# Layer 1 of a four-layer graph kernel: attending over the activations before the projection, logits from VectorE

## The reference, cut to what matters

```
h = relu(layernorm(x));  x = x + L0(h)    # deg*(h Wi + b) + A (h Wj)
h = relu(layernorm(x));  x = x + L1(h)
h = relu(layernorm(x));  x = x + L2(h)    # as L1, with W of 256x128; output and h W side by side
h = relu(layernorm(x));  x = x + L3(h)    # 8 heads: q, k, v, softmax, output projection

L1:  Wh = h W;  e_src = Wh a_src;  e_dst = Wh a_dst
     logits[n, m] = leaky_relu(e_src[n] + e_dst[m], 0.2), -inf where A[n, m] = 0
     out = softmax(logits) Wh
```

## Time and profile before

| | |
|---|---|
| median of 3 runs | 1220.35 us |
| the profiled execution | 1220.8 us |
| its span, first to last instruction | 1218.8 us |
| TensorE (PE) busy | 1200.7 us, 99% |
| ScalarE (ACT) busy | 1082.4 us, 89% |
| GpSimd (POOL) busy | 1068.4 us, 88% |
| VectorE (DVE) busy | 1053.9 us, 86% |
| granted TensorE clock, mean | 0.999 of full speed |
| DMA | 78.57 MB, 64 GB/s on average |

### The profile page before, as it was taken

The page is one execution under the profiler, slowest core; times in us unless marked ns, Lnnn a source line. Parts: engine busy times, 40 slices in busy tenths (PEclk is TensorE's granted clock), DMA queues, the critical chain, the costliest instruction groups (busy, mean ns, idle before and its releaser), DMA issues.

```text
span 1218.8 us, 43750 instructions
## 1 busy us (share of the span) xinstructions
PE 1200.7 (99%) x12017; PEld 1108.6 (91%) x12017; DVE 1053.9 (86%) x5142; ACT 1082.4 (89%) x3976; POOL 1068.4 (88%) x1848
## 2 busy tenths in 40 slices
PE   8999999999999999999999999999999999999997
PEld 7789999999999999999999999999999999999986
DVE  6898898898898898888988988988988888988874
ACT  3679898898898898898998998998998998998997
POOL 5998899899899898999899899899899899898774
PEclk9999999999999999999999999999999999999999
DMA  7333333343442433534333332432433343330001
GB/s 187 63 46 51 77 68 55 79 67 57 77 67 57 77 67 55 79 64 60 77 63 60 77 65 58 75 68 59 71 69 60 69 67 66 67 51 26 20 20 36
DMA packets 97678, 78.57 MB, mean 64 GB/s; under 512 B 31648, under 2 KB 89248, under 8 KB 97440
## 3 DMA queue, kind: packets, MB, share of 16 engines
q1 hardware_dynamic: 94960, 74.07, 32.9%
q10 hardware_dynamic: 2480, 1.71, 0.5%
HBM read 58.79 MB, written 16.95 MB: 62 GB/s over the span
## 4 chain that ended last, share of the span: by engine, by line
PE 90%; issue 1%; DVE 1%; POOL 0%; ACT 0%; POOLq 0%; DVEq 0%; ACTq 0%
PE bank L1565 16%; PE bank L1567 16%; PE bank L1566 16%; PE bank L1715 9%; PE bank L1670 6%; PE bank L1575 6%; PE bank L1707 6%; PE bank L1727 5%; PE bank L1646 4%; PE bank L1662 3%; PE bank L1626 2%; POOL probs L469 0%; ACT exps L1315 0%; DVE masked L874 0%; PE bank L1654 0%
## 5 line engine op out<-in xcount | busy, mean ns | idle before, releaser
L1315 ACT ACTIVATE exps<-masked,nmax 128x128 f32<-128x128 f32 x1024 | 396.8, 393 | 0.9 <-DVE nmax L874 0.4
L469 POOL TENSOR_TENSOR probs<-exps,rsum 128x512 f32<-128x512 f32 x256 | 266.3, 1042 | 16.2 <-DVE rsum L882 15.7
L440 POOL TENSOR_SCALAR y<-x,nm,rstd 128x256 f32<-128x256 f32 x384 | 212.0, 560 | 31.5 <-issue 31.0
L874 DVE CUSTOM_DVE_ANT_0 masked<-bank,mask 128x128 f32<-128x128 f32 x1024 | 227.4, 284 | 0.8 <-PE bank L1707 0.5
L1315 ACT ACTIVATION_READ_ACCUMULATOR exps<-masked,nmax 128x1 f32 x1024 | 197.3, 193 | 0.0
L760 DVE BATCH_NORM_STATS2 stats<-x 128x6 f32<-128x256 f32 x512 | 190.4, 414 | 4.6 <-DMA x<-in_x 4.4
L1565 PE MATMUL bank<-w_hi,ht_hi 128*128 128x512 f32 (+1 forms) x508 | 189.4, 373 | 0.4 <-DVE ht_lo L821 0.3
L417 POOL TENSOR_TENSOR rstd<-veps,power 128x2 f32<-128x2 f32 x256 | 182.7, 714 | 5.3
L1567 PE MATMUL bank<-w_hi,ht_lo 128*128 128x512 f32 (+1 forms) x508 | 172.6, 340 | 0.0
L1566 PE MATMUL bank<-w_lo,ht_hi 128*128 128x512 f32 (+1 forms) x508 | 172.5, 340 | 0.0
L1323 ACT ACTIVATE probs3t<-bank 128x512 f32<-128x512 f32 x256 | 145.0, 595 | 0.7 <-PE bank L1715 0.7
(11 more groups left out here) (136 smaller groups left out, 3970.4 us busy)
## 6 DMA issues: line engine op xcount, KB each, us to landing
x<-in_x SPq DMA_DIRECT2D x64, 256.0 KB, 5.9
xt_sb<-in_xt SPq DMA_DIRECT2D x64, 256.0 KB, 5.7
out<-x SPq DMA_DIRECT2D x64, 256.0 KB, 5.7
db<-rows SPq DMA_DIRECT2D x110, 128.0 KB, 4.1
mean_b<-rows SPq DMA_DIRECT2D x62, 128.0 KB, 3.4
rows<-dst SPq DMA_DIRECT2D x110, 1.0 KB, 3.6
rows<-mv SPq DMA_DIRECT2D x62, 1.0 KB, 5.8
probs<-in_w0t ACTq DMA_DIRECT2D x1, 256.0 KB, 3.5
```

The lines of the kernel that those rows point to most:

```text
L440: last = pool.tensor_scalar(y[i][:, b, g], src[:, bx, g], nm[i][:, s, g:g + 1], rstd[i][:, s, g:g + 1], ALU.add, ALU.mult)
L469: pool.tensor_tensor(probs3[:, p % BUFFERS["probs3"], j], exps3[:, p % BUFFERS["exps3"], j], rsum3[:, s, j].unsqueeze(2).to_broadcast([P, ...
L874: last = dve.tensor_tensor_reduce(masked3[:, b, j, i], bank_of(f"sc{j}")[:, i * P:(i + 1) * P], mask[:], scale=-1.0, scalar=-MASKED, op0=A ...
L1315: last = act.activation(exps3[:, b, j, i], masked3[:, p % BUFFERS["masked3"], j, i], ACT.Exp, bias=nmax3[:, s, j, i:i + 1], scale=-1.0, ac ...
```

## The change

Layer 1 is computed the other way round. GpSimd makes y1 = max(x1 - mean, 0), not yet divided by the deviation (`centre1`, which does not wait for `rstd1`). W a_src and W a_dst are made once, as rows spread over all partitions, in PSUM bank 6, which nothing else uses from then on. VectorE takes each node's two logits as dot products of y1 with these rows (`logit_products1`, 4 instructions of 256 columns, each with a running sum), GpSimd multiplies the 4 columns by the inverse deviation (`scale_logits1`), and SyncE sends the a_dst part from there. The exps are scaled by the inverse deviation of the neighbour as ScalarE copies their transposed form (`copy_exp_transposed1`, now two instructions of 128 columns). TensorE multiplies y1 by them, 4 products of 128 columns whose result is already transposed (`aggregate1`, g1), ScalarE and VectorE split it, and TensorE multiplies by w1, 12 products of 256 columns (`project1`). The transposition of y1, the copies to `wh` and the gather of `dst` for layer 1 are gone. The key bias moves from VectorE to ScalarE (`add_key_bias`, 2 instructions). x1 and y1 get a third buffer. The orders of all engines, the LAG table and the banks are new; the rotating banks are 0 to 5.

```diff
-    "h1t": (6, "h1t", ('h1t_lo',)),
-    "x3b": (4, "x3_mm", ('x3',)),
-    "sc3": (4, "scores", ('nmax3_3',)),
+    "g1": (3, "g1_mm", ('g1_lo',)),
+    "x3b": (1, "x3_mm", ('x3',)),
+    "sc3": (1, "scores", ('nmax3_3',)),
+        a1_rows = bank[6]
...
+            def centre1(p):
+                b, s, bx = p % BUFFERS["y1"], p % SMALL, p % BUFFERS["x1"]
+                passed(pool, "nm1", p)
+                read_before(pool, "y1", p, "dots1", "g1_mm")
+                for g in range(G):
+                    last = pool.tensor_scalar(y[1][:, b, g], x1[:, bx, g], nm[1][:, s, g:g + 1], 0.0, ALU.add, ALU.max)
+            def scale_logits1(p):
+                passed(pool, "dots1", p)
+                passed(pool, "rstd1", p)
+                passed(pool, "z1", p, SMALL)
+                pool.tensor_tensor(logits1[:, s], dots1[:, s], rstd[1][:, s].unsqueeze(1).to_broadcast([P, 2, G]), ALU.mult).then_inc(S["sd1"], 1)
...
+            def logit_products1(p):
+                passed(dve, "y1", p)
+                dve.wait_ge(S["products"], 1)
+                for g in range(G):
+                    for k in range(2):
+                        last = dve.tensor_tensor_reduce(products1[:, k, g], a1_rows[:, k * D:(k + 1) * D], y[1][:, b, g], scale=1.0, scalar=0.0,
+                                                        op0=ALU.mult, op1=ALU.add, accum_out=dots1[:, s, k, g:g + 1])
...
-            def copy_projection1(g, p):
-                act.activation(wh[:, b, g], bank_of(f"wh{g}")[:, 0:D + 2], ACT.Copy).then_inc(S[f"wh{g}"], 1)
+            def high_g1(p):
+                act.activation(ht1_r[0][:, b].rearrange("p c g n -> p (c g n)"), bank_of("g1")[:], ACT.Copy).then_inc(S["g1_hi"], 1)
+            def copy_exp_transposed1(p):
+                for g in range(G):
+                    last = act.activation(at[1][:, b, g], bank_of("at1")[:, g * P:(g + 1) * P], ACT.Copy, scale=rstd[1][:, s, g:g + 1])
+            def add_key_bias(p):
+                for c in range(DC):
+                    last = act.activation(kt[:, b, c], bank_of("kt")[:, c * G * P:(c + 1) * G * P], ACT.Identity, bias=bk_sb[:, c:c + 1])
...
+            def aggregate1(p):
+                passed(pe, "at1", p)
+                bank_free(pe, "g1", p)
+                for c in range(DC):
+                    for g in range(G):
+                        last = pe.matmul(bank_of("g1")[:, (c * G + g) * P:(c * G + g + 1) * P], y[1][:, b, g, c * P:(c + 1) * P], at[1][:, bt, g],
+                                         start=True, stop=True)
...
-                for c in range(DC):
-                    last = split_matmul(bank_of(f"wh{g}")[:, 0:D + 2], [h_[:, b, c, g] for h_ in ht1_r], [w_[:, c, :] for w_ in w1_r],
-                                        c == 0, c == DC - 1)
+                for g in range(G):
+                    for c in range(DC):
+                        last = split_matmul(bank_of("x2b")[:, g * D:(g + 1) * D], [h_[:, b, c, g] for h_ in ht1_r], [w_[:, c, :] for w_ in w1_r],
+                                            c == 0, c == DC - 1)
```

More of the change, by code:

```diff
@@ L287, in fill @@
                 load(3)
+                load(4)
                 write_means(2)
@@ L290, in fill @@
                 spread_means(2)
-                load(4)
                 write_means(3)
@@ L368, in _ @@
             fill()
-            for t in range(17, NP + 12):
+            for t in range(15, NP + 10):
                 step(t)
@@ L701, in _ @@
             fill()
-            for t in range(9, NP + 4):
+            for t in range(6, NP + 2):
                 step(t)
@@ L1194, in _ @@
             fill()
-            for t in range(11, NP + 6):
+            for t in range(11, NP + 7):
                 step(t)
@@ L1283, in sum_logits @@
                         logits = db[i][:, p % 2].rearrange("p (n g) -> p g n", g=G)[:, g]
-                    last = act.activation(bank_of(f"zz{i}")[:, (G + g) * P:(G + g + 1) * P], logits, ACT.Prelu, bias=src[:, bs, g, col:col + 1], alpha=SLOPE)
+                    last = act.activation(bank_of(f"zz{i}")[:, (G + g) * P:(G + g + 1) * P], logits, ACT.Prelu, bias=own[:, g:g + 1], alpha=SLOPE)
                 last.then_inc(S[f"z{i}"], 1)
@@ new lines, in fill @@
+                copy_projection2(1)
+                sum_logits(2, hh[:, (1) % BUFFERS["hh"], :, F1], 1)
+                copy_exp_transposed1(3)
+                high_mj(1, 6)
+                relu_transposed_high(3, ht3_r, last_of("kt_mm", "qt_mm", "v_mm"), 0)
+                exps(2, "rsum2", 1)
+                high_mj(0, 6)
+                high_g1(3)
+                add_key_bias(0)
+                copy_exp_transposed(2, 1)
+                relu_transposed2(2)
+                sum_logits(1, logits1[:, (4) % SMALL, 0], 4)
@@ new lines, in step @@
+                if due(t, "exp3_2"):
+                    exps3_of(2, t - LAG["exp3_2"])
+                if due(t, "exp2"):
+                    exps(2, "rsum2", t - LAG["exp2"])
+                if due(t, "z1"):
+                    sum_logits(1, logits1[:, (t - LAG["z1"]) % SMALL, 0], t - LAG["z1"])
+                if due(t, "kt"):
+                    add_key_bias(t - LAG["kt"])
+                if due(t, "at2"):
+                    copy_exp_transposed(2, t - LAG["at2"])
+                if due(t, "ht2"):
+                    relu_transposed2(t - LAG["ht2"])
@@ L1647, in project2, with spread_dst @@
                 last.then_inc(S["hh_mm"], 1)
-            def spread_dst(i, src, buffer, ready, col, p):
-                b = p % BUFFERS[buffer]
+            def spread_dst(i, own, ready, p):
                 passed(pe, ready, p)
@@ new lines, in fill @@
+                project0(0, 8)
+                project_transposed("qt", wq_r, 2)
+                project_transposed("kt", wk_r, 2)
+            def drain():
+                transpose_p3(0, NP - 4)
+                transpose_p3(3, NP - 4)
+                transpose_exp(2, NP - 1)
+                transpose_p3(1, NP - 3)
+                attend(2, hh, "hh", F1, NP - 1)
+                scores(NP - 2)
+                attend3(NP - 4)
+                project_v(NP - 2)
+                transpose_y(3, NP - 1)
+                transpose_p3(2, NP - 3)
@@ L1878, in step @@
             def step(t):
+                if due(t, "d1") and at_an_end(t - LAG["d1"]):
+                    spread_dst(1, logits1[:, (t - LAG["d1"]) % SMALL, 1], "sd1", t - LAG["d1"])
+                if due(t, "g1_mm"):
+                    aggregate1(t - LAG["g1_mm"])
+                if due(t, "h2t"):
+                    transpose_y(2, t - LAG["h2t"])
+                if due(t, "e2t"):
+                    transpose_exp(2, t - LAG["e2t"])
+                if due(t, "pt3"):
+                    transpose_p3(3, t - LAG["pt3"])
+                if due(t, "pt0"):
+                    transpose_p3(0, t - LAG["pt0"])
+                if due(t, "x3_mm"):
+                    attend(2, hh, "hh", F1, t - LAG["x3_mm"])
+                if due(t, "hh_mm"):
+                    project2(t - LAG["hh_mm"])
+                if due(t, "scores"):
+                    scores(t - LAG["scores"])
+                if due(t, "ot_mm"):
+                    attend3(t - LAG["ot_mm"])
+                if due(t, "x2_mm"):
+                    project1(t - LAG["x2_mm"])
+                if due(t, "v_mm"):
+                    project_v(t - LAG["v_mm"])
+                if due(t, "pt2"):
+                    transpose_p3(2, t - LAG["pt2"])
+                if due(t, "s0"):
+                    aggregate(t - LAG["s0"])
+                if due(t, "h3t"):
+                    transpose_y(3, t - LAG["h3t"])
+                if due(t, "pt1"):
+                    transpose_p3(1, t - LAG["pt1"])
+                if due(t, "e1t"):
+                    transpose_exp(1, t - LAG["e1t"])
                 if due(t, "m1"):
```

1277 lines of the change are left out of this document (587 added, 690 removed), and 26 rows, old and new, of the table LAG.

## The result

The changed kernel takes 1240.44 us (median of 4 runs, 1239.01 to 1244.67) against 1220.68 us for the kernel before in the same session: a ratio of 1.0167 with the 95% interval [1.0141, 1.0194]. It is 1.7% slower. The forecast was 1199 us with a range of 1190 to 1213. The profiled execution took 1239.31 us, its span 1237.2.

What follows compares the result with a forecast made beforehand. TensorE was taken to set the pace, at 18.36 us a step. Span 1218.8 - 26.2 (steps) + 1.0 (prologue) + 4 (fill and drain) = 1197.6 us, which gave a time of 1199 us, range 1190 to 1213.

Steps and rivals of the forecast that it cites:

- GpSimd, per pair: GpSimd's list per pair: gather gone, four-column product added, y1 unchanged in size; loop 17.7 us, between 17.5 and 18.0.
- VectorE's dot product: VectorE, layer 1's logits: 0.34 us each, between 0.21 and 0.42; four make 1.36 us per pair.
- (b): Rival: the time stays, needing a step of 18.3 us or fill and drain longer by 20 us; chance 0.06.
- Hand-offs: Waits between engines: all fit, the a_dst row included, so nothing was charged in steady steps.
- the margin that the prediction named: At the scores after layer 2's attention, whose bank VectorE must first empty: 0.2 to 0.3 us, taken as existing already.
- The term that I had at +4: Fill and drain: 3 us for dot products in the fill, 1 for ScalarE in the drain; +4 us (0 to 10).
- What TensorE saves in all: TensorE, per pair: -0.41 us, making the step 17.95 us; 64 pairs give -26.2 us.
- (a): Rival: the other engines set the pace, by GpSimd's loop or late ScalarE; step 18.1 us, time 1208 us; chance 0.21.
- (c): Rival: with bank 6 given away, TensorE waits for six rotating banks; decides from 0.41 us per step, 1249 us; chance 0.09.
- (d): Rival: VectorE's dot products slow it, from 0.73 us each on; at 0.8 us the time is 1242 us; chance 0.04.

Runs made afterwards that it cites:

- e1: The changed kernel with layer 1's y1 in the old `add, mult` form on GpSimd, layer 1's ReLU left out: 1223.03 us.
- e11: The changed kernel, slow `max` form kept, with SyncE issuing the load of x ahead of the writing of layer 2's row: 1232.01 us.
- e8: e1 with SyncE issuing the load of x ahead of the writing of layer 2's row: 1214.75 us.
- e10: e8 with the key bias moved back from ScalarE to VectorE, right behind the query bias: 1240.41 us.
- e6: The changed kernel with layer 1's y1 on ScalarE, two `Relu` activations a pair with the negative mean as bias: 1250.37 us.
- e9: The changed kernel with y1 split, GpSimd centring graph 0 and ScalarE graph 1, and x loaded ahead of layer 2's row: 1225.61 us.
- e3: The changed kernel with layer 1's y1 made on VectorE, in front of its dot products: 1272.69 us.
- e5: The changed kernel with extra instruction forms on GpSimd and VectorE behind its last pair, timed singly and together; no kernel time given.

## Why the prediction was wrong

The step that failed is in "GpSimd, per pair": "The y1 line has the same size." The size is the same, and the form is not. I had the duration of `add, mult` and gave it to `add, max`, without bounds of its own, on the engine that I had just found to have the least slack. The rows gave no upper end for it. I looked for the nearest row and two ends where VectorE's dot product was concerned, and not here. The form adds 2 x (1154 - 557) = 1.19 us per pair to my 17.7. The run shows a loop of 18.28, so the rest of the list was shorter than I had it, about 17.1. That was luck: idle time of GpSimd's own ahead of its y instructions fell from 31.0 us in all to 10.8, and ahead of x3_tail from 10.2 to 0.7, where I had counted on little more than the second. With the 17.7 the step would be 18.9. A step of 18.3 is that of rival (b), to which I gave 0.06; with the stalls and the deeper pipeline on top the time went past it.

The distance from the forecast, 1240.4 - 1199.2 = 41.2 us, by the runs:

- The `max` form: 17.4 us (after to e1). By the cut spans about half of it is in the loop (1013.2 to 1004.9) and half in the start (120.4 to 112.7); e11 to e8 shows the same, 121.0 to 113.1. In the second 60 us GpSimd is at 54.70 with the slow form and at 55.60 without, so it has little room in either; the chain through the start was not followed.
- The late rows: 8.3 us (e1 to e8). In "Hand-offs" the a_dst row "takes 3.6 us out and 4.1 us back and has some 12 us". For layer 1's row the 12 us hold (11.8), and though it takes 5.1 out it was never late. The late one is layer 2's, which has 9.0 us and stands nowhere in the prediction. Its medians are 3.8 and 3.8, and they say nothing of the ten spreads over 6 us. Nor had I asked what shares the queue with it. The reordering of SyncE's list was in the change, and I charged it nothing.
- The step: 18.13 on average in e8 against 17.99, and with the 55 steps of the cut 7.8 us. About 0.07 of the 0.15 in an unstalled step is at the scores. From layer 2's projection to the next transposition it was 0.90 us, and from there to the scores 0.56, of which 0.12 was waiting. Now the scores follow the projection directly, at 1.09. Before, and then in e8:

```profile
702.84 1.06 PE L1646 MATMUL bank<-w_sb,ht 128*128 128x130 f32 x8
703.74 0.60 PE L1575 MATMUL bank<-ident,y 128*128 128x128 f32 x4
704.30 1.17 PE L1707 MATMUL bank<-kt,qt 32*128 32x128 f32 x32
```

```profile
723.09 1.06 PE L1676 MATMUL bank<-w_sb,ht 128*128 128x130 f32 x8
724.18 1.17 PE L1736 MATMUL bank<-kt,qt 32*128 32x128 f32 x32
```

  That is the margin that the prediction named and took for kept. The rest is hundredths in several places, such as 1.44 for the 12 query products where the earlier trace rows has 1.41; I did not trace it further.
- Start and end: 215.4 us in e8 against 208.1, 7.3 more than forecast. The term that I had at +4 is thus +11, just over its upper end of 10. This is with the cheap form; in after the two ends are 224.0. I saw the extra step of depth and used it under (b) only; "Against: the drain's whole idle time is 9.2 us" compares it with the wrong thing. The end grew by a step (84.4 to 102.4). The start became shorter by 9.2 with the cheap form and by 1.9 with the slow one. My reading is that it gives back the whole step only if the other engines fill the pipeline faster; no run has the old depth.

Right were: the price of TensorE's new products (0.89 us for the four of `aggregate1`, forecast 0.90), the dot product (0.34 to 0.35, with the bound from the earlier trace rows and the increment from the earlier trace rows), the `at` copies (0.31) and nearly the key bias (0.81 for two, forecast 0.74), VectorE's and ScalarE's totals (16.9 and 17.0 us per pair in e8, forecast 16.8 and 17.3), and that GpSimd has the least slack. What TensorE saves in all was not right: of the 0.41 us a step about 0.25 is left in e8 (18.36 to 18.11), and its busy time is 1185.4 us there and not near 1175. On the Trainium skill's rule that an add belongs on VectorE (ScalarE: Activation LUTs, Rules for kernel authors): e10 decides for this kernel, and it is the other way by 25.7 us, not because of the instruction's price but because of what stands behind it. Of the rivals, (a) had the right engine and too small a size. (c), with the bank given away, did not happen at its size: of TensorE's waits for a bank in the steady part only the one at the scores shows, 0.07 us a step more than before where 0.41 would have decided. (d) did not happen either, though e10 shows how near it was.

Whether the extra step of depth was needed at all was not tried.

## What to carry to other kernels

An instruction with the same shape on the same engine is a new instruction if its operations differ: give it bounds of its own, and do it first on the engine with the least real slack, which is the length of its list when it never waits and not its busy share. Before a step is shortened, set the room of each hand-off against its latest arrivals and not against their median, for the hand-offs that the change leaves alone too, and look at what shares the queue: layer 2's row had 9.0 us for a median of 7.5 and was late in 15 of 55 steps. And work moved to an engine with room should not stand ahead of the instruction that the pacing engine is waiting for: e6 and e9 differ there by one activation of 0.4 us per pair, and by 0.33 us in the step.

## What the runs showed of the hardware

- GpSimd's two-operation form on 128x256 float32: `add, mult` 475 ns (column and immediate) to 558 (two columns), a single `mult` or `max` about 850, `add, max` 1154, 1235 with a column in place of the immediate, `max, add` with two columns 1217.
- A `tensor_scalar` of VectorE (subtract, max, with a column operand) from and to on-chip memory excludes GpSimd and is excluded by it: 326 to 1442 ns per instruction in e3 (0.27 us from start to start when alone, e5), and 11.41 us for one of GpSimd's behind forty of VectorE's.
- The spreading of a 1 KB row into 128 KB landed in 4.1 us as a rule (4.4 in e8), and in up to 8.6 us in after, 8.5 in e8 and 9.0 in e11, so with the 256 KB load between the row's transfers or not. The writing of the row took 3.8 and 5.1 us with the load near it on the queue and 3.1 and 3.0 us without (after and e8).
- TensorE's granted clock was 1.00 in the steady windows of both kernels. In the first two windows of 60 us it was 0.94 and 0.97 in after, where TensorE was idle 15.3 and 7.0 us, and 0.97 and 1.00 before, with 7.6 and 1.1 us idle; what that costs was not separated from the idling itself.
